# Wide attention: TensorE's loop over 64 groups of tokens written out straight

## The chip, the cores and the metric

The kernel runs on one core of one Trainium2 chip. The metric is the device time of one launch in microseconds (us), lower is better. TensorE (PE) multiplies, VectorE (DVE), ScalarE (ACT) and GpSimd (POOL) work element by element, SyncE (SP) issues the transfers. Each engine runs a program of its own, and they meet at semaphores.

## The reference

Four cross-attention layers follow one another on 16 batches of 128 tokens of width 256. The change lies in the first, "wide" layer (L0), which attends twice with 16 heads of width 128 and one extra bias key, and ends in a feed-forward:

```python
def _cross_attention(q_in, kv_in, wq, bq, wk, bk, wv, bv, wo, bo, bias_k, bias_v):
    qh = (q_in @ wq + bq).reshape(b, q_len, H, K)      # H = 16, K = 128
    kh = (kv_in @ wk + bk).reshape(b, t, H, K)
    vh = (kv_in @ wv + bv).reshape(b, t, H, K)
    kh = jnp.concatenate([kh, jnp.broadcast_to(bias_k, (b, 1, H, K))], axis=1)
    vh = jnp.concatenate([vh, jnp.broadcast_to(bias_v, (b, 1, H, K))], axis=1)
    logits = jnp.einsum('bqhk,bthk->bhqt', qh, kh) / scale
    weights = jax.nn.softmax(logits, axis=-1)
    ctx = jnp.einsum('bhqt,bthk->bqhk', weights, vh).reshape(b, q_len, H * K)
    return ctx @ wo + bo
...
res = x
x = res + _cross_attention(_layer_norm(x, ln1_scale, ln1_offset), xf_1, wq1, ...)
res = x
x = res + _cross_attention(_layer_norm(x, ln2_scale, ln2_offset), xf_2, wq2, ...)
h = _layer_norm(x, ln_mlp_scale, ln_mlp_offset)
return x + gelu(h @ w_fc1 + b_fc1) @ w_fc2 + b_fc2
```

L1, L2 and L3 (narrow heads, packed or masked attention, feed-forwards) follow; their code is the same in both kernels.

## The kernel before

**Tiling.** The two wide attentions are one run of 64 groups. A group is four batches (GROUP = 4, 512 tokens) of one pair of heads; four groups make a pair (GROUPS = 4), eight pairs an attention (PAIRS = 8). So groups 0 to 31 are the first attention and 32 to 63 the second. Every matrix product with weights is made as three products of float32r parts (`product3`, lines 768 to 774). TensorE's part of a group is in `pairs()` at line 843: for each of the group's four batches b it makes the scores (line 885), turns the probabilities of the batch before (line 895), projects queries, keys and values of the *next* group between them (`project`, lines 772 to 774), multiplies probabilities and values (line 909), and makes the output product of the batch two before. ACT copies the turned probabilities (line 1451), takes exponentials (1456) and the heads' high parts (1463). DVE takes the maxima (1850), the reciprocals (1855), scales the probabilities (1857), copies queries (1821) and values (1827), takes the heads' low parts (1869) and adds to x (1882). POOL splits the weights of the next pair (2382, 2420, 2424), and SP loads the weights of the pair after that (2635 to 2647) once POOL is done with the buffer.

**Order of the work.** Nothing is planned: each engine's program stands in the order of the Python code, and waits on semaphores whose counts grow with the group's number. `over_groups` (line 303) calls an engine's `window` once per group, in one of two ways. `fixed` writes the groups out one after another, with counts known when the program is built. `looped` writes one body of eight groups (span = 2 * GROUPS, two pairs) inside a loop of the engine, with counts worked out in registers from the loop's counter:

```python
    looped(1, last // 2 - span + 1)                            # groups 1 to 24: 3 rounds of 8
    fixed(last // 2 - span + 1, last // 2 + span + 1)          # groups 25 to 40
    looped(last // 2 + span + 1, last - span + 1)              # groups 41 to 56: 2 rounds of 8
    fixed(last - span + 1, last)                               # groups 57 to 63
```

The groups in the middle are written out because the second attention's normalization is threaded into groups 29 to 32 (`second_group`). PE, ACT and DVE each call `over_groups` (lines 932, 1471, 1894); POOL and SP go over the pairs in loops of their own. TensorE's loops jump back three times in all: from group 8 to 9, from 16 to 17, and from 48 to 49. After the 64 groups come the wide feed-forward (PE loop of line 983) and the three later layers, with loops on every engine.

Of the kernel before, what the change touches and what calls it, by code (L numbers as in the profile page):

```python
# [299 lines left out]
    return pair + k // GROUPS  # L300


def over_groups(engine, window, between):

    span = 2 * GROUPS
    last = 2 * PAIRS * GROUPS

    def fixed(first, end):  # L310
        for g in range(first, end):
            window(g, (g - 1) % span + 1, (g - 1) // span * 2, True, True, g + 1 < last)

    def looped(first, end):
        with engine.Fori(0, (end - first) // span) as i:
            for k in range(1, span + 1):
                window(span * i + (first - 1 + k), k, 2 * i + first // span * 2, True, True, True)

    window(-1, -1, 0, False, False, True)
    between(0)  # L320
    window(0, 0, 0, True, False, True)
    between(1)
    looped(1, last // 2 - span + 1)
    fixed(last // 2 - span + 1, last // 2 + span + 1)
    looped(last // 2 + span + 1, last - span + 1)
    fixed(last - span + 1, last)
    window(last, span, last // GROUPS - 2, False, True, False)


# [131 lines left out]
def program(nc, t, out, outer):  # L461
# [307 lines left out]
    def _(pe):  # L769
# [65 lines left out]
        def pairs():  # L835
# [35 lines left out]
            def window(g, k, pair, core, carry, following):  # L871
                gg = g
                ready, turning = second_group(g, 2), second_group(g, 1)
                for b in range(GROUP):
# [54 lines left out]
                    if not core and carry and b == 0:  # L929
                        turn_hidden(0)  # L930

            over_groups(pe, window, last_group)

        def turn_placed(b):
            pe.wait_ge(packed.placed, 2 * (b + 1))
# [428 lines left out]

        norm_and_split()
        pairs()
        feed_forward(0)
        layer1()
# [6 lines left out]
    def _(act):  # L1375
# [55 lines left out]
        def pairs():  # L1431
# [10 lines left out]
            def window(g, k, pair, core, carry, following):  # L1442
                gg = g
                turning = second_group(g, 1)
                for b in range(GROUP):
# [22 lines left out]
                    if turning is not None and b in (1, 2):  # L1468
                        split_half(turning, b - 1, b)

            over_groups(act, window, last_group)

        def split_hidden_weights(first, end):
# [235 lines left out]
    def _(dve):  # L1709
# [107 lines left out]
        def pairs():  # L1817
# [25 lines left out]
            def window(g, k, pair, core, carry, following):  # L1843
                gg = g
                ended = second_group(g, 0)
                for b in range(GROUP):
# [44 lines left out]
                    if core and not following:  # L1891
                        first_hidden(b)

            over_groups(dve, window, last_group)
            dve.wait_ge(x_added, 8 * PAIRS * 2 + ADD_CREDIT)

# [890 lines left out]
```

## Time and profile before

| what | us |
|---|---|
| time, median of 3 runs | 2366.11 (2364.85 to 2368.05) |
| span of the profiled execution, first to last instruction | 2360.4 |
| the runs' times over that span | 4.4 to 7.6, median 5.7 |
| PE matmul busy | 2185.3 (93% of the span) |
| DVE busy | 1779.8 (75%) |
| ACT busy | 1447.8 (61%) |
| POOL busy | 712.9 (30%) |
| mean granted TensorE clock | 0.969 of full speed |

The profiled execution has no time of its own beside its span; what lies around the span (start and end of the launch) is taken as the 5.7 us of the third row. Every time in the rows below is counted from the start of the span. Matmuls overlap in the records, so a busy PE is not a PE at its peak; what counts is the time at which each piece of a group starts, and the gaps.

### The profile page before, as it was taken

The page shows a single profiled execution, that of the slowest core. Times are in us where ns is not written, and L with a number is a line of the kernel's source. Part 1 is how long each engine was busy: PE and PEld are TensorE (multiplying, and loading weights), DVE is VectorE, ACT ScalarE, POOL GpSimd, SP SyncE. Part 2 cuts the span into 40 slices and gives each one's busy share as a digit, 9 for nine tenths or more (in the row PEclk, how much of TensorE's full clock was granted, in tenths as well). Part 3 has the DMA queues.
Part 4 walks back from the last instruction along what each step waited for, and adds up shares of the span by engine and source line. Part 5 has one row for each costly group of instructions (what it writes and reads, how often), then busy time and mean ns, then how long its engine had stood idle before and what let it go on. Part 6 is the DMA issues. An engine that isn't in the chain of part 4 may idle for free. (4 is left out here: it accounts for less than half of the span.)

```text
span 2360.4 us, 52377 instructions
## 1 busy us (share of the span) xinstructions
PE 2185.3 (93%) x17289; PEld 1771.2 (75%) x17289; DVE 1779.8 (75%) x4688; ACT 1447.8 (61%) x4010; POOL 712.9 (30%) x995
## 2 busy tenths in 40 slices
PE   5999999998999999998989999788999989899998
PEld 4898989997899989997986665455666669666664
DVE  6666666667766666666759999688899866799986
ACT  3555545554555555555656878567777766487875
POOL 1111111112311111100314655366676730244410
PEclk9999999999999999999998999799999999799999
DMA  5101010110010110000200000100000000000001
GB/s 130 23 23 25 24 24 19 41 24 23 20 27 23 24 23 8 17 1 4 67 5 10 11 11 6 38 8 1 4 14 18 15 8 3 6 13 9 9 4 37
DMA packets 72954, 47.28 MB, mean 20 GB/s; under 512 B 29232, under 2 KB 71600, under 8 KB 72752
## 3 DMA queue, kind: packets, MB, share of 16 engines
q1 hardware_dynamic: 72752, 44.62, 7.3%
q8 instruction: 123, 2.02, 0.3%
q14 instruction: 79, 0.65, 0.1%
HBM read 41.45 MB, written 2.10 MB: 18 GB/s over the span
## 5 line engine op out<-in xcount | busy, mean ns | idle before, releaser
L2009 DVE TENSOR_REDUCE maxima<-bank 128x2 f32<-128x512 f32 x512 | 333.0, 682 | 31.5 <-PE bank L1033 29.8
L1598 ACT ACTIVATE probs_t<-bank 128x512 f32<-128x512 f32 x512 | 282.8, 602 | 64.5 <-PE bank L1024 63.0
L1451 ACT ACTIVATE wide_probs_t<-bank 128x256 f32<-128x256 f32 x256 | 98.6, 385 | 301.8 <-PE bank L895 299.5
L1456 ACT ACTIVATE wide_probs<-bank,wide_neg_max 128x129 f32<-128x129 f32 x512 | 184.5, 365 | 120.5 <-DVE wide_neg_max L1850 116.6
L2382 POOL TENSOR_TENSOR wide_columns<-wide_pair_columns,zero 128x8 f32<-128x8 f32 x16 | 3.3, 206 | 739.1 <-DVE x L1882 695.4
L1855 DVE RECIPROCAL wide_inverse<-wide_sums 128x2 f32<-128x2 f32 x256 | 42.5, 166 | 226.4 <-ACT wide_probs L1456 226.4
L1463 ACT ACTIVATE wide_heads_high<-bank,wide_columns 128x128 fp32r<-128x128 f32 x512 | 160.5, 366 | 83.9 <-PE bank L909 82.3
L1857 DVE TENSOR_SCALAR wide_probs<-wide_probs,wide_inverse 128x128 f32<-128x128 f32 x512 | 177.4, 389 | 9.0
L1869 DVE SCALAR_TENSOR_TENSOR wide_heads_low<-bank,wide_columns,wide_heads_high 128x128 fp32r<-128x128 f32 x512 | 155.0, 344 | 35.1 <-ACT wide_heads_high L1463 30.3
L1634 ACT ACTIVATE probs<-scores_masked,neg_max 128x128 f32<-128x128 f32 x512 | 164.2, 395 | 26.9 <-DVE neg_max L2198 25.6
L1033 PE MATMUL bank<-k_packed,q_packed 32*128 32x256 f32 x1024 | 174.9, 340 | 3.7 <-ACT q_packed L1583 2.2
L1024 PE MATMUL bank<-q_packed,k_packed 32*128 32x256 f32 x1024 | 168.7, 332 | 8.4 <-ACT probs_t L1598 7.7
L909 PEld LDWEIGHTS bank<-wide_probs_t,wide_v 128*128 128x128 f32 x1024 | 150.0, 192 | 23.1 <-ACT wide_probs_t L1451 6.2
L772 PE MATMUL bank<-wide_weights_high,wide_heads_high 128*128 128x256 f32 x512 | 166.5, 325 | 0.0
L885 PE MATMUL bank<-wide_k,wide_q 128*128 128x129 f32 x1024 | 156.8, 275 | 6.4 <-issue 5.5
L1024 PEld LDWEIGHTS bank<-q_packed,k_packed 32*128 32x128 f32 x1024 | 105.1, 187 | 76.3 <-ACT probs_t L1598 38.3
L909 PE MATMUL bank<-wide_probs_t,wide_v 128*128 128x128 f32 x1024 | 157.9, 277 | 2.6 <-ACT wide_probs_t L1451 2.4
L885 PEld LDWEIGHTS bank<-wide_k,wide_q 128*128 128x128 f32 x1024 | 140.6, 191 | 13.2 <-issue 6.1
L772 PE MATMUL bank<-wide_weights_high,wide_ctx_high 128*128 128x256 f32 x512 | 148.1, 289 | 0.0
L773 PE MATMUL bank<-wide_weights_low,wide_heads_high 128*128 128x256 f32 x512 | 144.5, 282 | 0.0
L774 PE MATMUL bank<-wide_weights_high,wide_heads_low 128*128 128x256 f32 x512 | 144.5, 282 | 0.0
L773 PE MATMUL bank<-wide_weights_low,wide_ctx_high 128*128 128x256 f32 x512 | 142.9, 279 | 0.0
(311 smaller groups left out, 6829.2 us busy)
## 6 DMA issues: line engine op xcount, KB each, us to landing
cn<-in_ctx SPq DMA_DIRECT2D x48, 128.0 KB, 2.0
wide_pair_weights<-in_L_xattn_wq SPq DMA_DIRECT2D x16, 256.0 KB, 2.9
wide_pair_weights<-in_L_xattn_wk SPq DMA_DIRECT2D x16, 256.0 KB, 3.2
wide_pair_weights<-in_L_xattn_wv SPq DMA_DIRECT2D x16, 256.0 KB, 3.6
wide_pair_weights<-in_L_xattn_wo SPq DMA_DIRECT2D x16, 256.0 KB, 3.4
q_packed<-max_rows SPq DMA_DIRECT2D x256, 4.0 KB
wide_ctx_rows<-in_ctx SPq DMA_DIRECT2D x4, 512.0 KB, 6.9
x<-in_x SPq DMA_DIRECT2D x4, 512.0 KB, 8.0
```

The lines of the kernel that those rows point to most:

```text
L772: pe.matmul(acc, wh, mh, start=start, stop=False)
L773: pe.matmul(acc, wh, ml, start=False, stop=False)
L885: last = pe.matmul(wide_scores[b % 2][:, h * KEYS0:(h + 1) * KEYS0], q0[k % 2][:, h, b * P:(b + 1) * P], k0[k % 2][:, h, b, :], start=True ...
L909: last = pe.matmul(wide_heads[a % 2][:, h * P:(h + 1) * P], v0[parity][:, a, h * P:(h + 1) * P], probs_t0[:, a, h, :], start=True, stop=True)
L1024: last = pe.matmul(shifted_bank[j % 2][:, c * D:(c + 1) * D], k_packed[u][quad[a], pack, c * P:(c + 1) * P], q_packed[u][quad[a], pack, :] ...
L1033: last = pe.matmul(head_scores[packed_scores(1 - u, j)][:, c * D:(c + 1) * D], q_packed[1 - u][quad[b], pack, c * P:(c + 1) * P], k_packed ...
L1456: last = act.activation(probs0[:, b, h, :], wide_scores[b % 2][:, h * KEYS0:(h + 1) * KEYS0], ACT.Exp, bias=neg_max0[:, b, h:h + 1], accum ...
L1463: last = act.activation(heads_high[:, h, a, :], wide_heads[a % 2][:, h * P:(h + 1) * P], ACT.Identity, bias=columns[slot][:, 3, h:h + 1])
L1598: act.activation(probs_t[j % 8][:, :], shifted_bank[j % 2][:, :], ACT.Exp, bias=0.0).then_inc(s.exp_ready, 1)
L1634: last = act.activation(probs[t][:, part], scores_masked[t][:, part], ACT.Exp, bias=neg_max[t][:, h:h + 1])
L1857: last = dve.tensor_scalar(probs0[:, b, h, 0:P], probs0[:, b, h, 0:P], inverse0[:, b, h:h + 1], None, ALU.mult)
L2009: dve.tensor_reduce(maxima[pack // 2][:, b, pack % 2, :], head_scores[packed_scores(1 - u, j)][:, :].rearrange("p (a k) -> p a k", a=UNITS ...
```

## The change

`over_groups` takes a flag, and TensorE's call sets it: groups 1 to 63 then all come from `fixed`, and TensorE's part of the wide attention has no loop. ACT and DVE call it as before and keep both loops. What a window computes, and what it waits for, is the same.

```diff
-def over_groups(engine, window, between):
+def over_groups(engine, window, between, unrolled=False):
...
-    looped(1, last // 2 - span + 1)
-    fixed(last // 2 - span + 1, last // 2 + span + 1)
-    looped(last // 2 + span + 1, last - span + 1)
-    fixed(last - span + 1, last)
+    if unrolled:
+        fixed(1, last)
+    else:
+        looped(1, last // 2 - span + 1)
+        fixed(last // 2 - span + 1, last // 2 + span + 1)
+        looped(last // 2 + span + 1, last - span + 1)
+        fixed(last - span + 1, last)
     window(last, span, last // GROUPS - 2, False, True, False)
...
-            over_groups(pe, window, last_group)
+            over_groups(pe, window, last_group, unrolled=True)
```

How it moves TensorE's program is shown at two places. Repeats are shown with xN, waits that stand alone are not shown, and of the change the line numbers are three higher. The first place is the end of the first loop's body, that is of group 8, 16 and 24. Before:

```order
L772 MATMUL bank<-wide_weights_high,wide_heads_high 128x256
L773 MATMUL bank<-wide_weights_low,wide_heads_high 128x256
L774 MATMUL bank<-wide_weights_high,wide_heads_low 128x256
L315 REGISTER_ALU
L315 COMPARE_AND_BRANCH
L885 MATMUL bank<-wide_k,wide_q 128x129 x2
```

The L885 below the branch is group 25's; after group 8 and 16 the branch goes up to the body's top. The change, at the end of group 8:

```order
L775 MATMUL bank<-wide_weights_high,wide_heads_high 128x256
L776 MATMUL bank<-wide_weights_low,wide_heads_high 128x256
L777 MATMUL bank<-wide_weights_high,wide_heads_low 128x256
L888 MATMUL bank<-wide_k,wide_q 128x129 x2
L898 MATMUL bank<-ident,wide_probs 128x128 x2
```

The register step and the branch are gone, and group 9's scores stand right behind group 8's last product. The second place is the body's top, where group 9, 17 or 49 starts. Before (ISA and REGISTER_ALU rows work out the counts to wait for):

```order
L315 UNCONDITIONAL_BRANCH
L315 ISA
L883 ISA
L885 MATMUL bank<-wide_k,wide_q 128x129 x2
L895 MATMUL bank<-ident,wide_probs 128x128 x2
L850 ISA
L772 MATMUL bank<-wide_normed_high,wide_weights_high 128x512
L773 MATMUL bank<-wide_normed_low,wide_weights_high 128x512
L774 MATMUL bank<-wide_normed_high,wide_weights_low 128x512
```

With the change:

```order
L888 MATMUL bank<-wide_k,wide_q 128x129 x2
L898 MATMUL bank<-ident,wide_probs 128x128 x2
L775 MATMUL bank<-wide_normed_high,wide_weights_high 128x512
L776 MATMUL bank<-wide_normed_low,wide_weights_high 128x512
L777 MATMUL bank<-wide_normed_high,wide_weights_low 128x512
```

The products and their order are the same, and the register work between them is gone. TensorE's program grows from 6188 to 7998 such rows; those of the other engines stay.

## Rows read from the trace of the kernel before

**Rows 1.** Waits, 90 to 1010 us: engine line waited for: total us, times, longest.

```profile
PE bank L885 <- issue: 5.5, 3, 1.9
...
PE bank L774 <- issue: 1.6, 2, 1.3
```

**Rows 2.** Timeline of PE, first jump back: start, us, what, idle before and releaser.

```profile
203.96 1.02 PE L885 MATMUL bank<-wide_k,wide_q 128*128 128x129 f32 x4 [1.83 <-issue]
...
206.61 0.80 PE L774 MATMUL bank<-wide_normed_high,wide_weights_low 128*128 128x512 f32 x1 [0.35 <-issue]
```

**Rows 3.** The same, second jump back.

```profile
335.32 0.71 PE L885 MATMUL bank<-wide_k,wide_q 128*128 128x129 f32 x4 [1.89 <-issue]
...
337.98 0.79 PE L774 MATMUL bank<-wide_normed_high,wide_weights_low 128*128 128x512 f32 x1 [1.26 <-issue]
```

**Rows 4.** The same, third jump back.

```profile
874.70 0.71 PE L885 MATMUL bank<-wide_k,wide_q 128*128 128x129 f32 x4 [1.81 <-issue]
```

**Rows 5.** Timeline of PE: the first transposition of groups 5, 13, 21, 25.

```profile
139.47 0.44 PE L895 MATMUL bank<-ident,wide_probs 128*128 128x128 f32 x2 [1.27 <-DVE wide_probs L1857]
...
270.77 0.44 PE L895 MATMUL bank<-ident,wide_probs 128*128 128x128 f32 x2 [1.27 <-DVE wide_probs L1857]
...
404.51 0.44 PE L895 MATMUL bank<-ident,wide_probs 128*128 128x128 f32 x2 [1.27 <-DVE wide_probs L1857]
...
468.89 0.44 PE L895 MATMUL bank<-ident,wide_probs 128*128 128x128 f32 x2 [1.27 <-DVE wide_probs L1857]
```

**Rows 6.** The same of groups 41, 45, 53.

```profile
745.88 0.44 PE L895 MATMUL bank<-ident,wide_probs 128*128 128x128 f32 x2 [1.27 <-DVE wide_probs L1857]
...
810.24 0.44 PE L895 MATMUL bank<-ident,wide_probs 128*128 128x128 f32 x2 [1.27 <-DVE wide_probs L1857]
...
939.52 0.44 PE L895 MATMUL bank<-ident,wide_probs 128*128 128x128 f32 x2 [1.26 <-DVE wide_probs L1857]
```

**Rows 7.** Busy by stretch: PE, PEld, DVE, ACT, POOL, then granted clock, DMA share, GB/s.

```profile
203.96:206.26 2.30, 2.30 (x8) 1.58 (x8) 1.87 (x5) 0.78 (x4) 1.82 (x2) 0.55 0.05 14
206.61:208.00 1.39, 1.39 (x4) 1.16 (x5) 0.65 (x3) 0.07 (x1) 0.00 (x0) 0.64 0.58 175
...
337.98:344.30 6.32, 6.32 (x20) 5.45 (x21) 2.01 (x6) 0.64 (x3) 0.00 (x0) 0.51 0.68 180
```

**Rows 8.** The same behind the third jump back.

```profile
874.70:880.00 5.30, 5.30 (x35) 4.78 (x35) 4.11 (x12) 1.83 (x7) 1.86 (x2) 1.00 0.38 123
```

**Rows 9.** Timeline of DVE and ACT at group 9, after the first jump back.

```profile
201.60 2.19 DVE L1857 TENSOR_SCALAR wide_probs<-wide_probs,wide_inverse 128x128 f32<-128x128 f32 x2
...
205.41 0.42 DVE L1850 TENSOR_REDUCE wide_neg_max<-bank 128x2 f32<-128x258 f32 x1
205.44 0.39 ACT L1451 ACTIVATE wide_probs_t<-bank 128x256 f32<-128x256 f32 x1 [3.37 <-PE bank L895]
```

**Rows 10.** Timeline at group 5, where no engine jumps back.

```profile
137.23 2.19 DVE L1857 TENSOR_SCALAR wide_probs<-wide_probs,wide_inverse 128x128 f32<-128x128 f32 x2
...
139.95 0.39 ACT L1451 ACTIVATE wide_probs_t<-bank 128x256 f32<-128x256 f32 x1 [2.24 <-PE bank L895]
...
141.05 0.41 DVE L1850 TENSOR_REDUCE wide_neg_max<-bank 128x2 f32<-128x258 f32 x1
...
141.15 0.61 PE L909 MATMUL bank<-wide_probs_t,wide_v 128*128 128x128 f32 x4
```

**Rows 11.** Timeline of PE at the second attention's normalization.

```profile
572.34 0.44 PE L895 MATMUL bank<-ident,wide_probs 128*128 128x128 f32 x2 [1.84 <-DVE wide_probs L1857]
593.18 0.60 PE L895 MATMUL bank<-ident,wide_probs 128*128 128x128 f32 x2 [1.85 <-DVE wide_probs L1857]
614.01 0.44 PE L895 MATMUL bank<-ident,wide_probs 128*128 128x128 f32 x2 [1.85 <-DVE wide_probs L1857]
```

**Rows 12.** Busy by stretch there, columns as in rows 7.

```profile
560.00:600.00 40.00, 36.18 (x233) 32.17 (x232) 32.01 (x105) 21.40 (x72) 9.87 (x6) 0.91 0.00 1
```

**Rows 13.** DMA queue of instructions, 455 to 465 us: packets, MB, share.

```profile
q8 instruction: 1, 0.02, 0.8%
```

**Rows 14.** The same, 870 to 880 us, with the third jump back.

```profile
q8 instruction: 2, 0.03, 1.2%
```

## The prediction

> **What bounds the kernel now.** I read the table by engine first, then the waits of the wide attention, then TensorE's timeline around each place where its loops jump back, and last the timelines of DVE and ACT there. TensorE is the engine to watch: it is busy for 93% of the span, and in the wide attention (some 50 to 1100 us) it hardly stops. The waits of 90 to 1010 us put two lines of TensorE down to "issue", which is time in which it waited for no other engine: 5.5 us in three stalls before the scores and 1.6 us in two stalls before a projection [rows 1]. The timeline shows where they are. Three stand right at the jumps back, from group 8 to 9, from 16 to 17, and from 48 to 49: 1.83, 1.89 and 1.81 us before the first scores of the body [rows 2 to 4]. The other two, 0.35 and 1.26 us, come some 2.6 us later, in the middle of the body's first projection, after the first two jumps [rows 2, 3]. Nowhere in the 24 groups that are written out before is there such a stall, nor at the loops' starts and ends.
>
> The reader should also see the ordinary gap that lies at the same place of every pair: 1.27 us before the first transposition of group 4n+1, where TensorE waits for DVE's scaled probabilities [rows 5, 6]. DVE takes 2.19 us for the two halves there, while POOL splits weights [rows 9, 10]. This gap has nothing to do with the loop, and a stall of the loop takes its place where both meet.
>
> **What the change removes.** It takes TensorE's three jumps back away, with the register work of 40 groups; it adds no matmul, no wait and no transfer. The dearest way to count would be to add up the five stalls, 7.1 us [rows 1]. That is wrong on both sides: three ordinary gaps come back, and the clock is left out. So I measure by intervals between like points. An ordinary pair takes 468.89 - 404.51 = 64.38 us [rows 5] in a stretch that is nearly all loop body, and 810.24 - 745.88 = 64.36 us [rows 6]; I take 64.37. Two pairs are 128.74.
>
> - First jump: 270.77 - 139.47 = 131.30 [rows 5], 2.56 more.
> - Second jump: 404.51 - 270.77 = 133.74 [rows 5], 5.00 more.
> - Third jump: 939.52 - 810.24 = 129.28 [rows 6], 0.54 more.
>
> The sum is **8.10 us**. It can be rebuilt from its pieces. Each jump's stall less the ordinary gap that it replaces: 0.56, 0.62 and 0.54, together 1.72. The later stalls: 0.35 + 1.26 = 1.61 [rows 2, 3]. The rest is clock. After the first jump the granted clock is 0.55 over 2.30 us and 0.64 over 1.39 us, and after the second stall of the second jump 0.51 over 6.32 us; that is the lower of the two levels, 1.2 GHz, for most of these stretches, straight behind the idle time [rows 7]. The work lost is 2.30 x 0.45 + 1.39 x 0.36 + 6.32 x 0.49 = 4.6 us. After the third jump the clock stays at 1.00 [rows 8], and that jump costs only its 0.54. Pieces: 1.72 + 1.61 + 4.6 = 7.9, against 8.10 by intervals; I take 8.1, since it leaves nothing out.
>
> **Is all of it gained?** An ordinary gap of 1.27 us did not bring the clock down: the two transpositions behind it take 0.44 us in all seven rows [rows 5, 6], where behind a gap of 1.85 us and a fall they take 0.60 [rows 11]. With the stalls gone these gaps alone remain, so I expect no fall at the three places. The register work goes without a gain: a pair that is looped takes 64.36 us and one whose end is written out 64.38, so TensorE's program was not late inside a body. TensorE's gain passes on, as DVE, ACT, POOL and SP wait for TensorE's or each other's progress; the weights of a pair are loaded two pairs ahead.
>
> What was hidden beneath TensorE's stall are the jumps of DVE and ACT, which stay, and at the same groups. DVE does not notice its own: from the start of its slow scaling to group 9's maxima it takes 205.41 - 201.60 = 3.81 us [rows 9], and at group 5, without any jump, 141.05 - 137.23 = 3.82 us [rows 10]. So its next step came on time and costs 0. ACT is less certain. It copied group 9's turned probabilities at 205.44, when TensorE let it [rows 9]; without the stall it would be asked at about 201.60 + (139.95 - 137.23) = 204.32, 1.1 us sooner. If it were not ready then, TensorE would feel it only at L909, whose start is 141.15, when the copy ended at 139.95 + 0.39 = 140.34: 0.81 us of slack [rows 10]. So ACT's jump costs between 0 and 1.1 - 0.81 = 0.3 us each, 0.9 us in three. I take 0, as DVE's jump, of the same kind and time, shows nothing.
>
> The code that is now fetched: around the third jump the queue of instructions moves two packets in 10 us, and in a stretch without a jump one [rows 13, 14]. The body of eight groups does not stay with the engine between rounds, but is fetched again. Written out, as many packets are needed, but in order. Bounds: below, 0 as in the 24 written groups; above, a stall of 1.26 us like the second one of rows 3 at each of some 40 packets. I take 0, the row of the same kind of code.
>
> The Trainium skill (Runtime: NRT & Kernel Launch, section Instruction fetch mechanics) says that fetching ahead is purely sequential, and that a taken branch whose target is not at hand waits for a transfer of the target's page. The trace agrees, with 1.81 to 1.89 us at each jump and a second packet beside it.
>
> **The sum.** The profiled span of 2360.4 becomes 2352.3. What lies around it, and the luck of a run's clock, is 5.7 us at the median, so the time goes from 2366.1 to **2358.0**. That is 0.34% less. A measurement of this kernel can tell about 0.2%, 4.7 us, from no change; so "faster" means below 2361.4.
>
> **The rivals.**
>
> *Only the stalls are gained, the clock's part is not.* Whether 1.8 us of idle time brings the clock down was a matter of luck already in this one execution: twice yes, once no [rows 7, 8]. In the executions that were timed the falls may have been fewer than in the profiled one. Without any fall the loop costs 1.72, and two later stalls of about 1.26 each in place of 0.35 and 1.26: 4.2 us. The time would be 2361.9, within 0.2%. Between the two lie one or two falls, at about 1.6 us each (the first jump: 1.5 us lost; the second: 3.1). For it: each fall depends on where in time the gap lies. Against it: three runs within 3.2 us leave no room for a very different sum in each.
>
> *The gain is given back at the next transitions.* Everything behind group 9 starts 2.6 to 8.1 us sooner. In the normalization of the second attention TensorE has three gaps of 1.84 and 1.85 us [rows 11], and in the 40 us of the first two the clock was at 0.91, so it fell for some 7 us [rows 12]. Another meeting of gap and clock there, or at the entry of a later layer, moves the time by 1.6 us either way. Two falls more leave 8.1 - 3.2 = 4.9: 2361.2.
>
> *Code comes late.* Written-out code needs a new packet about every group. If fetching ahead did not keep up at every second one of the 40 groups that were looped, it would cost 20 x 1.26 = 25 us, less the 8.1 gained: 2383, slower by 0.7%. It decides from 7 late packets on (7 x 1.26 = 8.8). Against it speak the 24 groups written out before, with no issue stall at all, and the later layers' long written-out stretches. Also here: TensorE's later loops stand at other places of the program, so one of them could now meet a stall that it did not have.
>
> *The jump itself is cheap.* Then the 1.8 us would belong to something else that begins with groups 9, 17 and 49 and stays, and the change would do nothing: 2366.1. Against it: the pairs' starts that no jump precedes, seven of them shown, have DVE's 1.27 us and no issue stall [rows 5, 6]. The Trainium skill (Advanced Engine Details and Errata, section Control Flow Timing) gives about 108 ns for a compare-and-branch; by that estimate three jumps are worth 0.3 us and the time would be 2365.8. The trace disagrees: its stalls are some seventeen times as long.
>
> *ACT's jump shows.* 0.9 us of the gain is lost: 2358.9. This lies within the forecast.
>
> **How the numbers follow.** Forecast, with or without ACT's part, 0.62. Only part of the clock's share in the timed runs 0.22; most of that is still a gain over 4.7 us, so two thirds of it count as faster. Given back by the clock elsewhere 0.12, half of it faster. Code late, or a later loop worse off, 0.03, of which 0.02 is slower. The jump cheap 0.01. Faster: 0.62 + 0.15 + 0.06 = 0.83; slower 0.02; the same 0.15. The range reaches up to the first rival's 2361.9 and a little of the second, 2362.2, and down to a run in which two clock falls fewer happen elsewhere, less a part: 2355.4.
>
> **What would show it.** In the profile after, TensorE's scores at group 9, 17 and 49 follow without an "issue" gap, and the first transposition waits 1.27 us for DVE, as in every pair; the intervals between these points are 64.4 us throughout; the granted clock is 1.00 there; the projections have no issue stall. DVE's and ACT's rows at group 9 look like those of group 5. I would be wrong if "issue" turned up at other places of the wide attention, if ACT's copy came later than 0.5 us behind the transposition, or if the stage were 8 us shorter and the end were not.

## The result, and the profile after

The change takes 2354.59 us (median of 5 runs, 2349.84 to 2356.92), against 2366.11 us for the kernel before in the same series (median of 5, 2363.14 to 2368.05). The ratio is 0.9949, with a 95% interval of 0.9937 to 0.9961: faster by 0.4 to 0.6%. The prediction was 2358.0 us with a range of 2355.4 to 2362.2. The direction was right, and the time lies 0.8 us below the range: the gain of 11.5 us at the medians was put at 8.1.

The profiled execution of the change has a span of 2355.2 us, and its own time is 2356.92: 1.7 us lie around the span. In every later execution of either kernel 1.7 to 1.8 us lie around it. So the profiled execution of before, with its span of 2360.4, was one of about 2362.1 us, and 4 us better than its median. One execution of a run below (N = 15), of 2685.32 us at a mean clock of 0.742 against 0.960 to 0.972 in its other eleven, is left out of every figure.

First the waits of the wide attention, for TensorE, of the change:

```profile
PE bank L898 <- DVE wide_probs L1860: 26.5, 21, 1.8
...
PE bank L775 <- DVE wide_q L1824: 0.4, 2, 0.2
```

Both lines with "issue" are gone [rows 1]. TensorE waits for DVE's probabilities 21 times in place of 17: the ordinary gap has come back where the stalls stood. TensorE's timeline at the first transposition of groups 5, 9, 17, 25 (compare [rows 2, 3, 5]):

```profile
137.27 0.44 PE L898 MATMUL bank<-ident,wide_probs 128*128 128x128 f32 x2 [1.26 <-DVE wide_probs L1860]
201.63 0.44 PE L898 MATMUL bank<-ident,wide_probs 128*128 128x128 f32 x2 [1.27 <-DVE wide_probs L1860]
...
330.37 0.44 PE L898 MATMUL bank<-ident,wide_probs 128*128 128x128 f32 x2 [1.27 <-DVE wide_probs L1860]
...
459.10 0.44 PE L898 MATMUL bank<-ident,wide_probs 128*128 128x128 f32 x2 [1.27 <-DVE wide_probs L1860]
```

The distances are 64.36, 128.74 and 128.73 us: an ordinary pair of 64.37 everywhere. And from group 37 on, to group 49 and to group 57 (compare [rows 4, 6]):

```profile
672.97 0.44 PE L898 MATMUL bank<-ident,wide_probs 128*128 128x128 f32 x2 [1.27 <-DVE wide_probs L1860]
...
866.07 0.44 PE L898 MATMUL bank<-ident,wide_probs 128*128 128x128 f32 x2 [1.27 <-DVE wide_probs L1860]
...
994.80 0.44 PE L898 MATMUL bank<-ident,wide_probs 128*128 128x128 f32 x2 [1.27 <-DVE wide_probs L1860]
```

Then the stretches behind the places of the three jumps (columns as in [rows 7, 8]; the figure after the five engines is the granted clock):

```profile
201.63:208.00 6.37, 6.37 (x37) 5.55 (x38) 4.82 (x13) 2.71 (x11) 1.97 (x2) 1.00 0.45 141
330.37:344.30 13.93, 13.93 (x97) 12.85 (x98) 9.28 (x27) 7.50 (x27) 1.96 (x2) 1.00 0.48 97
866.07:880.00 13.93, 13.93 (x97) 12.85 (x98) 9.28 (x27) 7.50 (x27) 1.96 (x2) 1.00 0.38 96
```

The clock is at 1.00 in all three, and the last two stretches do the same number of matmuls in the same time. Last, DVE and ACT at group 9 (compare [rows 9, 10]):

```profile
199.38 2.19 DVE L1860 TENSOR_SCALAR wide_probs<-wide_probs,wide_inverse 128x128 f32<-128x128 f32 x2
...
202.11 0.39 ACT L1454 ACTIVATE wide_probs_t<-bank 128x256 f32<-128x256 f32 x1 [2.24 <-PE bank L898]
...
203.21 0.42 DVE L1853 TENSOR_REDUCE wide_neg_max<-bank 128x2 f32<-128x258 f32 x1
203.31 0.61 PE L912 MATMUL bank<-wide_probs_t,wide_v 128*128 128x128 f32 x4
```

ACT copies 0.48 us after the transposition, as at group 5 before (139.95 - 139.47), although both engines have just jumped back here. Their jumps cost TensorE nothing that shows.

Yet the two spans differ by 5.2 us only. By stages, with the points read from the timelines (us; "g5" is the first transposition of group 5, "layer 1" the first matmul of line 1072):

| stage | before | the change | difference |
|---|---|---|---|
| start to g5 | 139.47 | 137.27 | -2.2 |
| g5 to g29 (jumps 1 and 2) | 393.85 | 386.27 | **-7.6** |
| g29 to g37 | 148.19 | 149.43 | +1.2 |
| g37 to g57 (jump 3) | 322.37 | 321.83 | **-0.5** |
| g57 to layer 1 | 226.8 | 228.0 | +1.2 |
| layer 1 to the end | 1129.7 | 1132.4 | +2.7 |

Between these two executions the loops gave 8.1 us, as the intervals had said. The other stages together took 2.9 us more, which lies within the scatter of single executions: the ten profiles taken below in which the later layers' loops are left as they are range from 1126.2 to 1132.4 in the last row. So two questions were left: what do the jumps cost in other executions, and is there any gain outside them?

### The profile page after: what moved, and what is told of

Read it like the earlier page. It is cut to its first block and busy times, and to the rows that moved or that the text cites. A ratio compares the mean times of both kernels' runs of the same rounds, so it can differ in the third digit from the quotient of the medians.

```text
span 2355.2 us, 51956 instructions
## 1 busy us (share of the span) xinstructions
PE 2184.1 (93%) x17289; PEld 1770.4 (75%) x17289; DVE 1779.9 (76%) x4688; ACT 1445.0 (61%) x4010; POOL 712.6 (30%) x995
## 5 line engine op out<-in xcount | busy, mean ns | idle before, releaser
L1056 PE MATMUL bank<-probs_t,vn 128*32 128x256 f32 x2048 | 142.1, 396 | 1.2 <-DVE max_rows L1980 0.6
```

Source lines behind the costliest of these rows:

```text
L1056: last = pe.matmul(sum_bank[quad[m], :], v[:, c, PACK * g + m, :], probs_t[(PACK * g + m) % 8][:, c * D:(c + 1) * D], start=c == 0, stop=c ...
```

## The experiments

Jump costs below are read in the same way in each profile: g5 to g29 above 386.21 us, and g37 to g57 above 321.80 us, the lengths without a jump. Runs of one series share their runs of before.

**The kernel before, three times more.** No edit. What was expected of each:

> The kernel before, unchanged, once more. Asks how much its executions differ, and how much of that is TensorE's clock. If the 11.5 us measured between the two kernels are stalls and clock falls behind the jumps back, the span of an execution follows its mean granted clock: about 2360 us at 0.969, and the typical execution of 2366 us has a lower clock, near 0.964. The interval from group 5's first transposition to group 57's without the normalization is then longer than the first profile's by 1.6 us per further fall. If the clock has nothing to do with it, executions of 2363 and of 2368 us show the same mean clock. The stalls of 1.8 us stand at the three jumps again either way.

> The kernel before once more, for another profile. So far its three jumps back cost 8.2 and 10.1 us by the intervals (groups 5 to 29 above 386.2 us, groups 37 to 57 above 321.8), and the measured gain of the change is 10.7 us between the means. If the typical execution loses 10 to 11 us there, this profile shows 9 to 12; if the gain has another part outside the wide attention, it shows about 8 again.

> The same once more: 9 to 12 us if the jumps are the whole gain, about 8 if they are not.

| profile of before | own time | jumps 1 and 2 | jump 3 | sum |
|---|---|---|---|---|
| the first | about 2362.1 | 7.6 | 0.6 | 8.2 |
| e1 | 2363.44 | 9.1 | 1.0 | 10.1 |
| e9 | 2365.23 | 8.7 | 0.6 | 9.3 |
| e10 | 2361.43 | 9.4 | 1.1 | 10.5 |

The first profile had the cheapest jumps of the four; their mean is 9.5 us. An execution's own time does not tell which it is: e10 is the shortest of the four and has the dearest jumps, and e9, the longest, lies near the mean. The stalls vary: in e10 the second and third jump read

```profile
336.18 1.23 PE L885 MATMUL bank<-wide_k,wide_q 128*128 128x129 f32 x4 [2.32 <-issue]
339.13 0.80 PE L774 MATMUL bank<-wide_normed_high,wide_weights_low 128*128 128x512 f32 x1 [0.45 <-issue]
...
876.46 0.71 PE L885 MATMUL bank<-wide_k,wide_q 128*128 128x129 f32 x4 [2.38 <-issue]
```

against 1.89, 1.26 and 1.81 [rows 3, 4]. The four scores of 1.23 us at 336.18, against 0.71, are at the lower level of the clock (granted 0.50 from 336.18 to 338.60 us). All 83 executions of before in this study have a mean of 2365.4 us (single ones from 2360.1 to 2372.2). The four profiled ones are 2.3 us shorter than that on average, so whether 9.5 us is typical is not shown. The expected tie between a run's mean clock and its time is there but loose: the 12 runs of e1 have clocks from 0.964 to 0.973, with 2367.0 us at 0.964 and 2360.2 at 0.973.

**The change once more.**

> The change, unchanged, once more. The gain was 11.5 us at the medians and 8.1 by the intervals of the one profile. If 8.1 was right and the rest luck, this comes out nearer to 2358; if typical executions of the kernel before lose more behind their jumps than the profiled one did, it comes out at 2353 to 2356 again. No issue stall of TensorE in the wide attention in either case.

Measured: median 2356.19 us of 7 (mean 2355.0), ratio 0.9955 (0.9939 to 0.9971), no issue stall. With the first five, 12 executions have a mean of 2354.7 us. The gain between the means is 10.7 us, with a standard error of 0.8. The jumps of the four profiles explain 9.5 of it; the other 1.2 can't be told from chance.

**Loops that never jump back.** Each eight groups stand in a loop of one round:

```diff
     if unrolled:
-        fixed(1, last)
+        for first in range(1, last // 2 - span + 1, span):
+            looped(first, first + span)
+        fixed(last // 2 - span + 1, last // 2 + span + 1)
+        for first in range(last // 2 + span + 1, last - span + 1, span):
+            looped(first, first + span)
+        fixed(last - span + 1, last)
```

> The groups that were looped stand in five loops of a single round each, so every group is entered through a loop, with its compare-and-branch, but nothing jumps back. If the jump back is what costs, this is as fast as the change (2353 to 2357) and shows no issue stall before the scores. If entering a loop, its branch instruction or its register work costs, the stalls of 1.8 us stay at the five loops' ends and the time is near 2366.

Measured: median 2353.73 us of 6, ratio 0.9955 (0.9937 to 0.9972), g5 to g29 386.27 us, no issue stall. The compare-and-branch instructions still stand in TensorE's built program, and are never taken. So entering and leaving a loop costs nothing that shows, only the jump back does. The register arithmetic was folded to constants in such loops, so this run says nothing of it.

**Only the first loop written out.**

```diff
-        fixed(1, last)
+        fixed(1, last // 2 + span + 1)
+        looped(last // 2 + span + 1, last - span + 1)
+        fixed(last - span + 1, last)
```

> Only the first loop (groups 1 to 24, two jumps back) is written out; the second (groups 41 to 56, one jump) stays. By the profile of before the first two jumps cost 7.56 of the 8.10 us and the third 0.54; so nearly the whole gain should be here, 2354 to 2356, with one stall of 1.8 us left at group 49. If every jump costs the same in a typical execution, a third of 11.5 us is left out: about 2358.5. If the gain comes from something that the whole change does elsewhere, such as where the later loops stand in the program, any time up to 2366 is possible.

Measured: median 2364.28 us of 12, ratio 0.9991 (0.9977 to 1.0005). This was a miss: two of three jumps were gone, and hardly any gain. TensorE's timeline at group 49 of this run has the cause:

```profile
868.41 0.37 PE L890 MATMUL bank<-wide_k,wide_q 128*128 128x129 f32 x1 [2.24 <-issue]
871.10 0.80 PE L890 MATMUL bank<-wide_k,wide_q 128*128 128x129 f32 x3 [2.32 <-issue]
```

The one jump left has two full stalls, the second among the four matmuls of the first scores, and costs 6.1 us where it had cost 0.6 to 1.1. Its code is the same; only its place in the program is new. (By the means this run lies 8.6 us above the change; the 2.5 us that its profile does not explain stay open.)

In the built program TensorE's instructions can be counted, so its places can be worked out. The Trainium skill (Runtime: NRT & Kernel Launch, section Instruction fetch mechanics, and Advanced Engine Details and Errata, section ISA Cache) gives 256 instructions, 16 KB, to a piece that is fetched at once. The trace agrees: before, 2.02 MB come in 123 packets, and the change's 29 400 instructions or so come in 114, some 258 to a packet. The places that follow are estimates with that figure. I fitted one unknown, the number of instructions ahead of the kernel's own, from the place of the later stall of [rows 2]: 21 instructions into the first body a piece must end there, which gives 62. With it a piece ends 102 instructions into the second body in the kernel before, where no later stall is seen, and 6 into it in this run, just where the second stall stands. The fit was made after these stalls were seen; the next two runs test it on places chosen ahead.

**The place of the body, on purpose.** The kernel before, with N = 30 or 15 instructions ahead of TensorE's first work, so that pieces end 247 and 72 instructions into the two bodies (N = 30), or 6 and 87 (N = 15), in place of 21 and 102:

```diff
         def norm_and_split():
+            for _ in range(N):
+                pe.sem_inc(idle, 1)
             turn_context(0)
```

> The kernel before, with 30 instructions put at the very start of TensorE's program, which only raise a semaphore that nobody waits for, while TensorE waits for its first transfer anyway. They move everything behind them by 30 places. Theory: a jump back costs one fetch of code, and a second one if the fetched piece of the program ends soon behind the body's start; before, that was 21 instructions behind it for the first loop, and in the run with only the first loop written out 6 behind it for the other, which cost a second stall of 2.32 us. Moved by 30, the pieces should end 247 and 72 instructions behind the two bodies' starts. Then the stalls of 1.8 us before the scores stay, the later stalls are gone, the clock falls less, and the time is 2358 to 2362 against 2365. If the place in the program has no part in it, the later stalls stay and the time is 2365.

> As the one with 30, but with 15 instructions. By the theory the piece now ends 6 instructions behind the first body's start and 87 behind the second's: the first two jumps cost two full stalls (2.2 and 2.3 us, the second among the first scores) and more clock, some 6 us each in place of 4 to 5, and the third 0.5 to 1. The time is 2367 to 2370 against 2365. If the place has no part in it: 2365.

| | pieces end at | jumps 1 and 2 | jump 3 | median | ratio |
|---|---|---|---|---|---|
| before (four profiles) | 21, 102 | 7.6 to 9.4 | 0.6 to 1.1 | | |
| N = 30 | 247, 72 | 3.2 | 0.7 | 2361.86 | 0.9987 (0.9976 to 0.9998) |
| N = 15 | 6, 87 | 10.5 | 0.7 | 2366.47 | 1.0015 (1.0000 to 1.0029) |

With N = 30 the waits of 90 to 1010 us have one issue line for TensorE's matmuls, and with N = 15 one with five stalls; first the one, then the other:

```profile
PE bank L887 <- issue: 6.0, 3, 2.1
```

```profile
PE bank L887 <- issue: 10.8, 5, 2.6
```

The stalls stand where the theory put them. The sizes fit less well. By the profiles 5.6 us of the loops' mean cost of 9.5 go away by moving the same code 30 instructions (4.3 to 6.6 against the single profiles of before), and 1.7 come on top by moving it 15 (0.7 to 3.0). By the runs' means N = 30 is 3.3 us faster than before, and its median lies at the upper edge of the 2358 to 2362 expected. N = 15 is 2.8 us slower by the means; its median lies just under the 2367 to 2370 expected, and its first two jumps cost 10.5 us in place of some 12. In the times the effect is clear of noise for N = 30, and for N = 15 only just. Of N = 15 at the first jump:

```profile
202.38 0.37 PE L887 MATMUL bank<-wide_k,wide_q 128*128 128x129 f32 x1 [2.23 <-issue]
205.07 0.81 PE L887 MATMUL bank<-wide_k,wide_q 128*128 128x129 f32 x3 [2.32 <-issue]
```

These are, to 0.01 us, the stalls of the run with only the first loop written out, at another loop of another program, with the piece's end again 6 instructions in. At its second jump N = 15 has them at the same two matmuls, with 1.85 and 2.56 us.

**The later code at its old places.** The change, with 155 such instructions, 75 at the start and 80 ahead of the first feed-forward; the lines are those of the last diff.

> The change, with 155 such instructions (75 at the start, 80 ahead of the feed-forward, where TensorE waits for GpSimd), so that the code of the feed-forwards and of the later layers stands at the same places against the pieces of the program as in the kernel before. If the jumps back of the wide attention are the whole cause, the time is that of the change, 2354 to 2357. If part of the gain came from the new places of the later loops, that part is lost: up to 2358 and more. The 155 instructions themselves may cost up to 2 us if they are not hidden.

Measured: median 2367.01 us of 11, ratio 1.0004 (0.9993 to 1.0015). Taken by its time alone this would say that the whole gain came from the later loops' places. The stages say otherwise. Start to g5 takes 146.68 us, 7.4 to 9.4 more than in the two profiles of the change, and TensorE's first matmul waits:

```profile
12.47 3.65 PE L788 MATMUL bank<-ident,wide_ctx_rows 128*128 128x128 f32 x16 [12.47 <-issue]
```

The 75 instructions took the start of TensorE's program from 5.3 to 12.5 us and were not hidden: 7.2 us more are 0.10 us each, and with the 5.3 us that the engine would have waited anyway they are 0.17 at most. The 80 others made g57 to the feed-forward 125.65 us in place of 120.3, of which 2.9 came back up to layer 1. The wide attention's stages are those of the change (386.21 and 321.80), and from layer 1 to the end it takes 1132.2 us, against 1132.4 in both profiles of the change. So the places of the later code do nothing that shows. The instructions had been expected to cost up to 2 us; the run is no test of the time, and is of use by its stages only.

**More code written out.** First all of TensorE's loops (`fixed` for every batch in `over_batches` and `over_sequence`, a Python loop in place of `pe.Fori` in the feed-forward), then DVE's and ACT's `over_groups` beside TensorE's, and last all loops of the three engines.

> All of TensorE's loops written out, those of the two feed-forwards and of the three later layers too. The bodies there are shorter (108 to 755 machine instructions against 1966) and show no issue stall of TensorE at their jumps, so the theory expects little: 2352 to 2356, with up to 2.7 us less than the change where the packed attention's looped batches take 16.47 us each and its written-out ones 16.30. If every jump back costs 1.8 us, sixteen or so more are gone: 2340 or less.

> The change, with ACT's and DVE's programs of the wide attention written out as well. It asks whether their own jumps back, at the same groups, cost anything once TensorE's stall no longer covers them. In the profile of the change DVE's and TensorE's intervals are 64.37 us at every pair, so nothing should be left to gain: 2353 to 2356, the same as the change. If a jump of ACT or DVE still cost TensorE something outside the gaps looked at, 1 to 3 us less.

> TensorE, ACT and DVE without any loop in the whole kernel (GpSimd and SyncE keep theirs). TensorE alone gave 2351.4, with the first packed attention 6 us shorter (293.0 against 299.0 us). If ACT's and DVE's loops are as free as in the wide attention, this is the same, 2349 to 2353. If their jumps or register work hold up the short steps of the later layers, where DVE is busy for over 90% of some stretches, it is faster: down to 2335.

| loops written out | median (n) | ratio |
|---|---|---|
| TensorE, wide attention (the change, second series) | 2356.19 (7) | 0.9955 (0.9939 to 0.9971) |
| the same, and ACT and DVE there | 2353.75 (6) | 0.9954 (0.9937 to 0.9970) |
| TensorE, everywhere | 2351.38 (6) | 0.9941 (0.9925 to 0.9958) |
| TensorE, ACT, DVE, everywhere | 2349.02 (6) | 0.9928 (0.9915 to 0.9942) |

ACT's and DVE's loops in the wide attention are worth nothing that shows: g5 to g29 is 386.23 us without them. The third row lies just below the 2352 to 2356 expected, the last at the edge of the 2349 to 2353. The last row is faster than both kernels of this case. Its six runs, 2345.93 to 2349.30, all lie below the lowest of the change's twelve, 2349.84. Where in the later layers that gain lies I did not settle: in the profile of the third row layer 1 takes 293.0 us against 299.0, and in that of the last 296.1, while profiles of before give 297.6 to 299.7.

The queue that fetches TensorE's code supports the whole picture. Its lines on the profiles' pages, of the change, of the run with one jump left, and of TensorE without any loop:

```profile
q8 instruction: 114, 1.87, 0.3%
```

```profile
q8 instruction: 117, 1.92, 0.3%
```

```profile
q8 instruction: 141, 2.31, 0.4%
```

The three built programs fill 115, 108 and 142 pieces. Without a jump of the long body each piece but one is fetched once; with one jump left ten are fetched again, and in the kernel before, with 94 pieces, 123 packets and three jumps, thirty. The body of 1966 instructions fills 7.7 pieces.

## Why the prediction was right and wrong

**The cause was right.** The three jumps back of TensorE's loops cost the time, not the loop's entry (one-round run), not the register work (64.36 us a looped pair before, 64.36 to 64.37 the same pairs written out), and the code written out is fetched in time. The prediction read from one extra packet around a jump that the body is fetched again; thirty extra packets in the whole kernel bear it out. All signs named for the profile after are there: no issue stall, 1.27 us for DVE at each pair, 64.37 us throughout, the clock at 1.00 at the three places.

**The pieces of the sum.** "The sum is 8.10 us" held for the execution it was read from: 7.6 and 0.5 are what the two profiles differ by there. ACT's term of 0 to 0.9 us, taken as 0, measured 0: ACT came 0.48 us behind the transposition, and writing its loop out changed nothing that shows. Late code, taken as 0, measured 0. "It adds no matmul, no wait and no transfer" held: the ordinary gaps came back, as counted.

**The step that failed** is the main term, "The sum is 8.10 us", which one execution had given and which was taken for the typical cost of the three jumps. The mechanism was right and the term too small: the same three jumps, read in the same way, cost 9.3, 10.1 and 10.5 us in three further profiles, 9.5 in the mean of four, and the gain between the means is 10.7. "What lies around it, and the luck of a run's clock, is 5.7 us at the median" was wrong too: only 1.7 us lie around a span, so the profiled execution was 4 us shorter than the median. That does not account for the miss, since only 1.3 of these 4 us are jumps cheaper than the mean, and the even shorter e10 has the dearest ones. Of the 3.3 us between the forecast of 2358.0 and the change's mean of 2354.7, the jumps' term is 1.4, the starting time is 0.7 (the three runs' median of 2366.1 against the mean of 2365.4), and 1.2 stay open.

The first rival went wrong the same way round: it supposed that timed executions had fewer falls of the clock than the profiled one, with a gain of 4.2 us. They had more stall and more clock loss. The range had the same fault. Its lower end allowed for other stages, but for no jump dearer than those read, though the falls of the clock were known to depend on luck; as much room below the forecast as above it, 4.2 us, would have reached 2353.8. Its price was off as well: 1.6 us a fall fits the first jump (1.5), but the second had lost 3.1, so two falls were worth 4.6 us and not 3.2.

**The rivals.** Only the stalls gained: no. Given back at the transitions: part of the scatter, in either direction; the two profiles of the change are the highest there (1132.4 us), and their executions, 2356.9 and 2358.7 us, are themselves above the change's mean of 2354.7. Code late: no, 0 stalls in 63 groups. The jump itself cheap: no. The 108 ns that the Trainium skill (Advanced Engine Details and Errata, section Control Flow Timing) gives for a compare-and-branch are not what a jump back costs here, 1.8 to 2.4 us of stall each in four profiles of before. What a jump costs whose target is at hand no run shows. I had not thought of the later stalls as something that depends on where the body lies, though [rows 2, 3] had them at the same instruction twice, and [rows 4] not at all, which is what gives it away.

## What to carry to other kernels

A loop whose body is longer than what the engine keeps of its code pays for each jump back, and the price depends on where the body's start lies in the program: 0.6 us for one jump, 6 us for the same jump at another place. Write such a loop out, or look for "issue" stalls at the same instruction behind each jump, and move the body. And before a term read from one profile is carried to a median, read it in more profiles of the same kernel: here it was 8.2, 9.3, 10.1 and 10.5 us in four, and the length of an execution did not tell which of them it would be.

## What had not been expected

- With 30 idle instructions ahead of it the kernel before is faster by 3 to 4 us (2361.86 against 2365.63 at the medians), with no other edit.
- A full stall behind a jump takes 1.8 to 2.6 us. The clock falls at all eleven jumps that have two stalls. At the eight with a single one, of 1.8 to 2.4 us, it stays up in seven; the exception is the first jump of N = 30, which costs 2.25 us above the ordinary pair where 0.66 would be the stall's part:

```profile
204.39:206.40 2.01, 2.01 (x9) 1.82 (x10) 1.77 (x5) 0.59 (x2) 1.73 (x2) 0.62 0.06 16
```

- TensorE's shorter bodies, up to 795 instructions in the built program or some three pieces, jump back without fetching again: without a loop each piece is fetched once, and the kernel with one long-body jump left has only the ten extra fetches of that jump.
- An instruction that only raises a semaphore cost TensorE 0.10 to 0.17 us at the program's start, so 75 of them are not free even where the engine would wait 5.3 us. Thirty of them are: with N = 30 the first matmul starts at 5.62 us, as before.
